# One pass instead of two for the expert biases of a mixture layer, with the routes held twice

## The reference, cut to what matters

```python
h = relu(einsum('baf,efh->ebah', x, eW1) + eb1)      # 4 experts
h = relu(einsum('ebah,ehg->ebag', h, eW2) + eb2)
all_out = einsum('ebag,ego->ebao', h, eW3) + eb3
gates = softmax(x @ gW + gb)
topv, topi = top_k(gates, 2); topw = softmax(topv)
gated = sum(all_out[topi] * topw)
out = layernorm(x + shared_mlp(x) + gated)
```

## Time and profile before

| | before |
|---|---|
| median of 3 runs | 879.07 us |
| profiled execution, its own time | 881.01 us |
| its span | 879.2 us |
| PE busy | 838.2 us (95%) |
| DVE busy | 717.9 us (82%) |
| POOL busy | 524.4 us (60%) |
| ACT busy | 483.5 us (55%) |
| mean granted clock of PE | 0.99 |

### The profile page before, as it was taken

The page is one execution under the profiler, slowest core; times in us unless marked ns, Lnnn a source line. Parts: engine busy times, 40 slices in busy tenths (PEclk is TensorE's granted clock), DMA queues, the critical chain, the costliest instruction groups (busy, mean ns, idle before and its releaser), DMA issues.

```text
span 879.2 us, 23479 instructions
## 1 busy us (share of the span) xinstructions
PE 838.2 (95%) x9144; PEld 360.6 (41%) x9144; DVE 717.9 (82%) x1189; ACT 483.5 (55%) x782; POOL 524.4 (60%) x387
## 2 busy tenths in 40 slices
PE   5799999999999999999999997898999999999996
PEld 2134334344344343343343443464444444444442
DVE  5788888888888888888888888894788788788785
ACT  3646456455454464564554554358666566566562
POOL 2699999999999999999999964101121121121110
PEclk9999999999999999999999998999999999999999
DMA  9588998989989989999899764000000000000000
GB/s 374 158 240 252 260 283 245 263 267 260 275 250 260 286 242 259 278 250 263 256 253 264 217 168 111 2 2 2 0 13 13 25 13 13 25 13 13 25 13 36
DMA packets 70560, 141.60 MB, mean 161 GB/s; under 512 B 5440, under 2 KB 5440, under 8 KB 69440
## 3 DMA queue, kind: packets, MB, share of 16 engines
q1 hardware_dynamic: 70464, 140.21, 55.4%
HBM read 68.88 MB, written 4.19 MB: 83 GB/s over the span
## 4 chain that ended last, share of the span: by engine, by line
PE 39%; POOL 37%; issue 7%; DVE 7%; ACT 4%; DMA 3%; SPq 2%; POOLq 1%; DVEq 0%; ACTq 0%
POOL sb_rows L497 11%; POOL sb_prodv L604 7%; POOL sb_rows L502 6%; PE ring L1207 5%; POOL sb_wgt L592 4%; PE ring L1177 4%; POOL sb_rows L504 3%; POOL sb_score L586 3%; PE ring L952 3%; PE bank_ms L1219 3%; DMA sb_wbc<-sb_wgt 3%; SPq L545 2%; PE bank_ms L924 2%; PE qp L991 2%; PE qp L1162 2%
## 5 line engine op out<-in xcount | busy, mean ns | idle before, releaser
L952 PE MATMUL ring<-sb_arena,sb_wqkv 64*64 64x512 f32 x2048 | 254.1, 599 | 2.3 <-DVE sb_prodk L1349 1.5
L1380 DVE TENSOR_TENSOR sb_prodv<-ring,sb_wbc 128x1024 f32<-128x1024 f32 x128 | 151.8, 1206 | 43.6 <-DMA sb_wbc<-sb_wgt 25.4
L1349 DVE TENSOR_TENSOR sb_prodk<-ring,sb_qbuf 128x1024 f32<-128x1024 f32 x128 | 150.6, 1218 | 22.3 <-PE ring L952 16.8
L648 POOL TENSOR_TENSOR sb_parts_q<-sb_arena,sb_const 128x512 fp32r<-128x512 f32 x15 | 15.6, 1039 | 245.6 <-DVE sb_arena L1585 194.4
L497 POOL TENSOR_TENSOR sb_rows<-sb_arena 128x2048 f32<-128x2048 f32 x31 | 142.2, 4586 | 15.8 <-DVE sb_sum L489 15.8
L692 ACT ACTIVATE sb_xsq<-sb_arena 128x2048 f32<-128x2048 f32 x64 | 118.6, 1901 | 2.0 <-DMA sb_arena<-x 2.0
L952 PEld LDWEIGHTS ring<-sb_arena,sb_wqkv 64*64 64x64 f32 x2048 | 66.3, 132 | 115.6 <-issue 72.3
L991 PEld LDWEIGHTS qp<-sb_prodv,sb_tok_w 64*64 64x64 f32 x3072 | 93.1, 137 | 40.4 <-issue 40.2
L991 PE MATMUL qp<-sb_prodv,sb_tok_w 64*64 64x128 f32 x3072 | 98.8, 276 | 5.2 <-POOL sb_prodv L604 5.2
L604 POOL TENSOR_TENSOR sb_prodv<-sb_prodv 128x256 f32<-128x256 f32 x128 | 92.8, 735 | 10.7 <-DVE sb_prodv L1380 10.7
L663 ACT ACTIVATE sb_means<-sb_sum 128x256 f32<-128x256 f32 x32 | 13.3, 416 | 146.9 <-POOL sb_sum L507 143.1
(11 more groups left out here) (248 smaller groups left out, 1450.1 us busy)
## 6 DMA issues: line engine op xcount, KB each, us to landing
sb_arena<-x SPq DMA_DIRECT2D x64, 1024.0 KB, 7.4
sb_wbc<-sb_wgt SPq DMA_DIRECT2D x256, 256.0 KB, 5.7
out<-sb_arena SPq DMA_DIRECT2D x16, 256.0 KB, 2.0
sb_rest_w<-rest_w SPq DMA_DIRECT2D x1, 950.5 KB, 21.3
sb_const<-const SPq DMA_DIRECT2D x1, 264.5 KB, 3.0
sb_tok_w<-tok_w SPq DMA_DIRECT2D x1, 260.5 KB, 2.9
sb_const<-const SPq DMA_DIRECT2D x1, 256.0 KB, 21.6
```

The lines of the kernel that those rows point to most:

```text
L952: mm = pe.matmul(ring[slot][C * half:C * half + C, i, :], image_block(w, i), x[C * i:C * i + C, m, half, c], start=True, stop=True)
L1349: dve.tensor_tensor(by_pixel(prodk[:, c]), by_pixel(ring[c % 2][:, :, :]), q[:, :, None, :].to_broadcast([P, 2, N_PIX, G32]), ALU.mult).th ...
L1380: dve.tensor_tensor(prodv[:, :, :, G32 * c:G32 * (c + 1)], by_pixel(ring[k % 2][:, :, :]), by_pixel(wbc[:, c]), ALU.mult).then_inc(values_ ...
```

## The change

The biases' remainder no longer has a matrix of its own: the packed weights hold `eb3` on four row ranges, and rows 64 to 103 of `exact` are overwritten with the remainder. `route` holds its rows twice, at 0 to 39 and, from the new constant `TWICE`, at 64 to 103. One pass over 104 rows takes the place of the two over 40. The second copy is written by a new instruction of ACT (`double_routes`, high part, from SBUF) and a new one of DVE (low part, from PSUM). Both count on one new semaphore, `routing_doubled`, for which the bias pass and `out_rows` wait.

```diff
-            pool.tensor_tensor(b3_low[:, :], b3, exact[:, H_B3:H_SEL].bitcast(F32), ALU.subtract).then_inc(weights_split, 1)
+            pool.wait_ge(route_cleared, 1)
+            low = slice(TWICE, TWICE + N_ROUTE)
+            pool.tensor_tensor(exact[low, H_B3:H_SEL], b3[low, :], exact[low, H_B3:H_SEL].bitcast(F32), ALU.subtract).then_inc(weights_split, 1)
...
+            def double_routes(i):
+                act.wait_ge(routing_high, i + 1)
+                act.activation(route[TWICE:TWICE + 2 * E, :], route[0:2 * E, :].bitcast(F32), ACT.Copy).then_inc(routing_doubled, 1)
...
                     if live:
                         exp_logits(i)
+                    if i <= ITERS:
+                        double_routes(i - 1)
                     if behind:
                         out_sq(i - 2)
...
                 pe.wait_ge(routing_low, min(i + 2, ITERS))
+                pe.wait_ge(routing_doubled, 2 * min(i + 2, ITERS))
                 for g in range(G):
                     mm = pe.matmul(bank_base[:, g * P:(g + 1) * P], ysum[:, tokens_of(g)], centre, start=True, stop=True)
...
-            def bias_part(i, part):
-                if part == 0:
-                    pe.wait_ge(routing_low, i + 1)
-                    pe.wait_ge(sum_taken, i)
-                    if i + 1 < ITERS:
-                        wait_taken(pe, "expert1", i + 1, SIDE, 0)
-                by = exact[0:N_ROUTE, H_B3:H_SEL] if part == 0 else b3_low[0:N_ROUTE, :]
-                pe.matmul(bank_sum[:, :], by, route[0:N_ROUTE, :], start=(part == 0), stop=False, skip_group_check=True)
+            def routed_bias(i):
+                pe.wait_ge(routing_doubled, 2 * i + 2)
+                pe.wait_ge(sum_taken, i)
+                if i + 1 < ITERS:
+                    wait_taken(pe, "expert1", i + 1, SIDE, 0)
+                pe.matmul(bank_sum[:, :], exact[0:TWICE + N_ROUTE, H_B3:H_SEL], route[0:TWICE + N_ROUTE, :],
+                          start=True, stop=False, skip_group_check=True)
...
                 dve.tensor_tensor(in_order(route[LOW:LOW + 2 * E, :]), by_group(bank_base[0:2 * E, :]), in_order(high),
                                   ALU.subtract).then_inc(routing_low, 1)
+                dve.tensor_tensor(in_order(route[TWICE + LOW:TWICE + LOW + 2 * E, :]), by_group(bank_base[0:2 * E, :]), in_order(high),
+                                  ALU.subtract).then_inc(routing_doubled, 1)
...
-        for at in (0, LOW):
+        for at in (0, LOW, TWICE, TWICE + LOW):
             out[at + E * i:at + E * i + E, R_B3 + C * i:R_B3 + C * i + C] = a["L0_ffn_eb3"]
```

More of the change, by code:

```diff
@@ L61 @@
 N_ROUTE = LOW + 2 * E
+TWICE = 64
 SV_A, SV_S, SV_NM, SV_F, SV_FB, SV_CD, SV_NS, SV_G, N_SV = range(9)
@@ L158, in build @@
         exact = ctx.enter_context(nc.sbuf_tensor("sb_exact", [P, H_END], F32R))
-        b3_low = ctx.enter_context(nc.sbuf_tensor("sb_b3_low", [P, P], F32R))
         route = ctx.enter_context(nc.sbuf_tensor("sb_route", [P, CH], F32R))
@@ L299, in build @@
         routing_low = sem("routing_low")
+        routing_doubled = sem("routing_doubled")
         route_cleared = sem("route_cleared")
@@ L1251, in _ @@
                 if late:
-                    bias_part(i - 1, 0)
-                    bias_part(i - 1, 1)
+                    routed_bias(i - 1)
                     spread_routes(i - 1)
```

## The result

The changed kernel takes 931.95 us (median of 4 runs, 930.09 to 935.45) against 879.88 us of the kernel before on the same chip (879.07 in the table of before is the median of three of these four runs): the ratio is 1.059, 95% interval 1.057 to 1.061. The direction and the place were forecast, the size was not: 52 us in place of 26, outside the range of 898 to 910.

A forecast was written before the change was run, and what follows sets the result against it. PE, busy all 50 us of a window, sets the pace through its in-order list. Stalls 13 x 1.85 + 1.90, tail 0.36 and iteration 1's 0.1 sum to 26.4 us on the median 879.07: 905.5 us, range 898 to 910.

The forecast's parts named there:

- the chain PE, DVE, ACT, ACT, PE: `turn_logits`, DVE's work, exponentials, ACT's copy, then `out_rows`: each waits for the one ahead; before, only PE stood there.
- its 14 stalls: PE waits at `out_rows` for ACT's copy in iterations 2 to 15: 13 times 1.85 us, once 1.90.
- the place that has no cover: `out_rows` stands ahead of the experts' first matmuls on PE; its wait delays the whole rest of the iteration, nothing gives it back.
- the clock falls: Rival: each new stall lowers PE's clock behind it, 1.2 us lost each, 17 us on top, 922 us; 5%.
- My worked gap of 1.6 us: PE's new idle gap, from the end of L1149's matmul at 784.63 to `out_rows` at 786.2.
- DVE's second low part: Added DVE instruction behind L1618, starting 0.60 us later; mostly covered by DVE's idle time, 0.05 us left.
- ACT's copy: Copy behind `exp_logits`: starts 0.09 us before its predecessor's end, takes 0.63 us, its end reaches PE 0.05 us later.
- The removed pass: One of two bias passes a block on PE, 0.24 us, swallowed by a later wait: 0 in 15 iterations, 0.24 in the tail.
- the 104-row pass: Merged bias pass on PE, taken at the same 0.24 us as one over 40 rows, having the same 512 columns.
- waits no longer than before: Sign at PE's third spreading pass: wait for ACT's relu should grow to about 0.58 us; if not, the removed bias pass was worth its time.
- partly paid back: Rival: PE's later waits at L1198 and L1214 vanish, returning 0.62 us an iteration, 897 us; 7%.
- not held: Rival: PE is not stopped at `out_rows`, so only the saved bias pass counts, 875.5 us; 3%.

The follow-up runs named there:

- the second experiment: Kernel before plus ACT's copy and the wait of `out_rows` for it; both bias passes and the single low part stay: 910.04 us, 1.035.
- the fifth experiment: Changed kernel plus two matmuls that nobody reads, put into PE's gap ahead of the wait of `out_rows`: 912.32 us, 1.037.
- sixth: Kernel before plus ACT's copy, DVE's second low part and the wait of `out_rows` for both; the two 40-row bias passes stay: 933.75 us, 1.061.
- eighth experiment: Kernel before without the second bias pass, the one over the biases' remainder; nothing else changed: 880.22 us, 0.999.
- fourth: Changed kernel with the second copy of all 40 rows made by POOL from SBUF; nothing new on ACT or DVE, `out_rows` waits as before: 880.17 us, 0.999.
- tenth: Changed kernel with POOL making the second copy, and PE's two variance passes moved between the second and third spreading passes: 882.33 us, 1.002.

## Why the prediction was wrong

What bounds the kernel, the chain PE, DVE, ACT, ACT, PE, its 14 stalls and the place that has no cover: right. The wait alone, measured by the second experiment, costs 30 us; by its profile, whose span grew by 26.7 us, just what I forecast for all. That the two figures agree is luck: a stall of that kernel is 1.98 us long (783.00 to 784.98), where my terms without DVE's part add up to 1.80.

The step that failed is the rival "the clock falls", to which I gave 5% and 17 us on top. It came, and with 19.6 us (the fifth experiment against the changed kernel; 12 falls at 1.7 us are 20.4 by the clock column). I set it aside because after a gap of 1.66 us the clock had stayed at 1.00 and because 16 us of dense work stood between the gaps. The sixth and second experiments show how near that was: with gaps of 1.74 us the clock stays in the trace that I have, with 1.95 us it goes in most iterations. My worked gap of 1.6 us lay just on the good side, and the true one on the other. Its price was short as well. I read 2.4 us at the lower level from the earlier trace rows, which begin at 604; the window ahead of them in the kernel before is low too,

```profile
603.00:604.00 1.00, 1.00 (x9) 0.50 (x2) 0.00 (x0) 0.99 (x2) 0.00 (x0) 0.52 0.00 0
```

so that fall cost 1.7 us and not 1.2, just what one costs in the changed kernel. The rule that I quoted from the Trainium skill ("TensorE: Matmul & The Clock Gate", A second HAM failure mode: psum-queue depth-cycling) was the better guide: frequent short idles between groups of matmuls made the clock swing, here in 12 of 14 iterations at 1.7 us each.

The term that was mis-sized is the stall, 2.20 us in place of 1.85:

- DVE's second low part started 0.71 us behind the first and L1572 0.72 behind that; I had taken 0.60 from L1626. That is 0.22 us in place of 0.05. The right row was in my own list: L1618 at 849.39 and L1564 at 850.10 are 0.71 apart.
- ACT's copy started at 775.93, 0.03 us behind the end of L833 at 775.90, not 0.09 before it.
- From the copy's end at 776.56 to the load at 776.67 is 0.11 us, not 0.05; the tail had shown 0.12.

That is 0.35 us and 14 times 4.9 us. It matters twice, since these tenths carried the gap from a length at which no fall was seen to one at which most gaps had one. The sum with both repaired is 880 + 26.4 + 4.9 + 20.4 = 932, against 932; without the clock it is 911, and the fifth experiment took 912.3. The copy itself was sized right: 0.627 us against 0.63.

The removed pass: 0 forecast, 0 measured (eighth experiment). But I took the 104-row pass at the price of one over 40, and it costs a little more than both did (fourth and tenth experiments). So the wait of the third spreading pass went to 0.17 us, in the changed kernel too, where I had said about 0.58, and the sign by which I wanted to know that the pass was worth its time ("waits no longer than before") would have misled: the wait shrank and nothing was gained. The Trainium skill states what fits this (same page, Step-by-step: what each phase is for): weights are loaded ahead of running matmuls if their row groups do not conflict, or if they go to the background weight buffer. The 40 rows share row groups with only one of the two 64-row matmuls that run side by side ahead, the 104 rows with both, and their weights came 0.43 and 0.95 us behind the load ahead. That the row groups are the reason is argued, not shown: no run moved the rows.

The rivals "partly paid back" and "not held" did not occur; by the sixth experiment nothing came back.

## What to carry to other kernels

Before a counter is made to stand for two producers, ask what each waiter needs: here the PSUM bank's next writer waited for an SBUF copy that it had nothing to do with, and a semaphore of its own gave back 40 of 52 us. When a stall is put on TensorE, price its clock as well, and if the worked gap lies near one that the trace shows as harmless, put both cases in the range; a profile with the gap filled by idle matmuls (mind that a float32 one is two passes) tells the two costs apart. A matmul that is merged into one with more rows is not free because its column count stays: read when its weights can be loaded.

## What the runs showed of the hardware

The gap of 1.95 us in iteration 2 of the changed kernel did not lower the clock; the windows of that place:

```profile
634.00:636.00 2.00, 0.11 (x2) 0.00 (x0) 1.50 (x8) 1.45 (x3) 0.00 (x0) 1.00 0.00 0
...
638.00:640.00 2.00, 2.00 (x12) 0.97 (x10) 1.59 (x3) 1.49 (x3) 0.67 (x1) 1.00 0.00 0
640.00:642.00 2.00, 2.00 (x9) 0.57 (x5) 1.68 (x4) 1.60 (x4) 1.64 (x2) 1.00 0.00 0
```

The next ten gaps are 1.95 us too, and behind each of them the clock fell. Behind the one of iteration 13 it did not, with the same row ahead of the same work:

```profile
858.15 1.13 PE L1172 MATMUL qp<-sb_const,sb_arena 128*128 128x128 f32 x8 [1.95 <-ACT sb_route L841]
```

```profile
857.00:862.00 5.00, 3.85 (x22) 2.34 (x24) 2.37 (x8) 2.85 (x6) 0.58 (x1) 1.00 0.00 0
```

So near this length it is not the gap alone that decides. What else does is open. And the fall comes late: in the iteration shown above `out_rows` right behind the gap ran at the full 2.4 GHz, and the experts' matmuls 1.1 us later paid for it. The delay is not fixed either. Behind the gap that ends at 654.7 the clock is 1.00 until 655.0 and 0.54 on the mean from there to 656.0; behind the one that ends at 837.8 it is 1.00 until 839.0 and 0.70 in the us after. The slow rows of a profile need not be those next to the gap that caused them.
